# Recommender tower on one core: x_pair in 2 KB packets, chunk 0's loads together, a 128-row spread, idle transposes in two waits

## The chip, the cores and the metric

The kernel runs on one core of one Trainium2 chip. The metric is the device time of one execution in microseconds; the kernel before has a median of 543.13 us over 3 runs (542.85 to 1859.66). The profiled execution took 546.4 us, of which 544.6 us is the span from the first to the last instruction.

## What is computed

512 rows of 32 categorical fields are looked up in 32 tables of 16-wide fp32 embeddings. A compressed interaction network of three layers with 128 outputs each runs over them; its sums and 16 dense features go through three dense layers.

```python
e = jnp.stack([tbl_0[ids[:, 0]], ..., tbl_31[ids[:, 31]]], axis=1)      # (512, 32, 16)
x0, h = e, e
for i in range(3):
    z = (x0[:, :, None, :] * h[:, None, :, :]).reshape(B, F * G, E)
    y = relu(einsum('oc,bce->boe', Ws[i], z) + bs[i][None, :, None])
    if i != 2:
        x_keep, h = y[:, :64, :], y[:, 64:, :]
    else:
        x_keep = y
    xs.append(x_keep)
z = jnp.sum(jnp.concatenate(xs, axis=1), axis=2)
h = jnp.maximum(jnp.concatenate([z, dense_ctx], axis=1) @ W_top1 + b_top1, 0.0)
h = jnp.maximum(h @ W_top2 + b_top2, 0.0)
y = h @ W_top3
```

## The kernel before

The batch is cut into 16 chunks of 32 rows; a chunk's 32 rows times 16 components are the N = 512 columns of every big matmul. A layer of a chunk is a sum over channel products: VectorE (DVE) multiplies field tiles of x by h into z, TensorE (PE) multiplies z with the weights and adds up in a PSUM bank, ScalarE (ACT) applies relu and writes h for the next layer, twice (two halves of the partitions).

Layers 1 and 2 have 16 tiles of products (TILES), in 4 groups k of 4 tiles (GROUP). A step (layer, chunk, k) is one DVE product of 128x2048 and then the matmuls of its two pairs of tiles. A pair "by tensor" is two full fp32 matmuls (`unsplit`, L624), which the profile records as two records each: a whole step by tensor is 8 records. A pair in AT is split: ACT writes its high part (L520), GpSimd (POOL) its low part (L382), and PE runs six faster matmuls (`split`, L637). Layer 0 has one step per chunk, from x_rep and x_rot (L422). For chunk 0 nothing is split. PLAN lists the steps; every engine runs through it in this order. It begins with (1,0,0) to (1,0,3), (2,0,0), (2,0,1), (0,1,0), (2,0,2), (2,0,3), (1,1,0), (0,2,0), (1,1,1) to (1,1,3), and then turns through nine steps per chunk. The first steps of layers 1 and 2 of chunk 0 (HALVED) are made by DVE in two halves of 128x1024.

Data path of a chunk c: POOL issues 8 indirect gathers (L369) into `gathered`; SyncE (SP) stores them to `x_scratch` in DRAM (`store_x`, L295, two DMAs), and loads them back, replicated, as x_rep and x_rot for layer 0 (`load_x0`, L301 and L304, 5 DMAs of 256 KB over all 128 partitions) and as x_pair for layers 1 and 2 (`load_half`, L288). x_pair has two buffers, chunk mod 2. A group k of x_pair comes in two DMAs of 512 KB: half a = 0 goes to partitions 0 to 63, each of which gets the same four rows of x, half a = 1 to partitions 64 to 127 with four other rows. Since a group's four tiles stand side by side in a partition, each packet is 8 KB. All of SP's DMAs are written by hand in one order and go to one queue; the queue carries them out in that order.

The start is different. Chunk 0's gathered tile is loaded straight into `x_first`, which is 32 partitions of x_rot, and PE spreads it with five selecting matmuls (`spread_first`, L654) into PSUM; ACT copies the first bank to x_rep (L572), DVE makes the four product tiles of (0,0,0) from the banks (L461), and PE multiplies them (`start`, L660 and L664). Before it, PE turns the dense features (L669) and runs BUSY = 28 transposes of the identity that nobody reads (L677). Of chunk 0's x_pair, SP and ACT load the groups 0 and 1, one half each, as soon as store_x(0) has landed. SP then waits for chunk 1's gathers, stores chunk 1, and only then loads groups 2 and 3.

## Time and profile before

| what | us |
| --- | --- |
| median of 3 runs | 543.13 |
| profiled execution | 546.4 |
| its span | 544.6 |
| PE busy | 501.3 (92%) |
| DVE busy | 379.8 (70%) |
| POOL busy | 358.2 (66%) |
| ACT busy | 196.1 (36%) |

A busy PE is one with a matmul in flight. The page cuts the span into 40 slices of 13.6 us; the granted clock of TensorE is given in tenths of full speed. Times in the timeline are from the span's start.

### The profile page before, as it was taken

The page shows a single profiled execution, that of the slowest core. Times are in us where ns is not written, and L with a number is a line of the kernel's source. Part 1 is how long each engine was busy: PE and PEld are TensorE (multiplying, and loading weights), DVE is VectorE, ACT ScalarE, POOL GpSimd, SP SyncE. Part 2 cuts the span into 40 slices and gives each one's busy share as a digit, 9 for nine tenths or more (in the row PEclk, how much of TensorE's full clock was granted, in tenths as well). Part 3 has the DMA queues.
Part 4 walks back from the last instruction along what each step waited for, and adds up shares of the span by engine and source line. Part 5 has one row for each costly group of instructions (what it writes and reads, how often), then busy time and mean ns, then how long its engine had stood idle before and what let it go on. Part 6 is the DMA issues. An engine that isn't in the chain of part 4 may idle for free.

```text
span 544.6 us, 4268 instructions
## 1 busy us (share of the span) xinstructions
PE 501.3 (92%) x1446; PEld 273.1 (50%) x1446; DVE 379.8 (70%) x219; ACT 196.1 (36%) x253; POOL 358.2 (66%) x220
## 2 busy tenths in 40 slices
PE   0966769899999999999999999999999989899987
PEld 0622335355555555555545555555555554455555
DVE  1333964695959595959687786959595969867573
ACT  1210340434434443534253434334444424241242
POOL 5770347597969697887969696969697744715000
PEclk9897997999999999999999999999999999999999
DMA  7679599349998989797979797979798777350200
GB/s 230 131 164 255 150 243 233 105 110 250 219 247 184 250 182 238 167 235 160 228 158 231 166 227 161 221 166 243 159 220 199 171 196 159 89 110 9 76 0 0
DMA packets 33549, 94.50 MB, mean 174 GB/s; under 512 B 7844, under 2 KB 15012, under 8 KB 25080
## 3 DMA queue, kind: packets, MB, share of 16 engines
q1 hardware_dynamic: 27208, 91.87, 70.7%
q0 software_dynamic: 4096, 1.06, 1.7%
q10 hardware_dynamic: 2224, 1.31, 1.2%
q8 instruction: 11, 0.18, 0.2%
q14 instruction: 10, 0.08, 0.1%
HBM read 92.05 MB, written 2.10 MB: 173 GB/s over the span
## 4 chain that ended last, share of the span: by engine, by line
PE 75%; DVE 10%; issue 5%; DMA 4%; POOL 3%; ACT 2%; SPq 0%; DVEq 0%; ACTq 0%
PE acc L624 26%; PE acc L637 15%; PE spare L624 14%; PE x_bank L624 12%; DVE z L434 7%; PE x_bank L637 3%; POOL gathered L369 3%; PE spare L637 3%; DMA gathered<-in_table,rows_all 2%; DMA x_pair<-x_scratch 2%; DVE z L422 1%; DVE zl_parts L446 1%; DVE sum L451 1%; PE acc L642 1%; ACT h L534 1%
## 5 line engine op out<-in xcount | busy, mean ns | idle before, releaser
L382 POOL TENSOR_TENSOR z_low<-z,z_high 128x1024 fp32r<-128x1024 f32 x88 | 214.4, 2447 | 110.2 <-ACT z_high L520 109.4
L434 DVE TENSOR_TENSOR z<-h,x_pair 128x2048 f32<-128x2048 f32 (+1 forms) x65 | 144.8, 2248 | 115.8 <-ACT h L534 105.6
L624 PE MATMUL acc<-z,w_direct 128*128 128x512 f32 x384 | 175.0, 598 | 11.1 <-DVE z L434 11.1
L369 POOL DMA_INDIRECT gathered<-in_table,rows_all x128 | 143.6, 1122 | 33.3 <-issue 26.4
L520 ACT ACTIVATE z_high<-z 128x1024 fp32r<-128x1024 f32 x90 | 93.3, 1054 | 149.7 <-DVE z L434 127.7
L624 PEld LDWEIGHTS acc<-z,w_direct 128*128 128x128 f32 x384 | 72.9, 191 | 91.1 <-issue 71.9
L624 PE MATMUL spare<-z,w_direct 128*128 128x512 f32 x200 | 92.9, 603 | 11.2 <-DVE z L434 11.2
L624 PE MATMUL x_bank<-z,w_direct 128*128 128x512 f32 x200 | 89.9, 593 | 4.6 <-DVE z L434 4.6
L434 DVE TENSOR_TENSOR z<-h_odd,x_pair 128x2048 f32<-128x2048 f32 x32 | 72.3, 2278 | 8.1 <-ACT h_odd L534 8.1
L434 DVE TENSOR_TENSOR z<-h_even,x_pair 128x2048 f32<-128x2048 f32 (+1 forms) x33 | 72.3, 2213 | 5.2 <-ACT h_even L534 5.2
L624 PEld LDWEIGHTS spare<-z,w_direct 128*128 128x128 f32 x200 | 38.1, 193 | 55.6 <-issue 41.7
L624 PEld LDWEIGHTS x_bank<-z,w_direct 128*128 128x128 f32 x200 | 37.7, 189 | 44.4 <-issue 39.6
L637 PE MATMUL acc<-z_high,w_high 128*128 128x512 f32 x124 | 57.9, 548 | 0.0
L422 DVE TENSOR_TENSOR z<-x_rep,x_rot 128x2048 f32<-128x2048 f32 x15 | 44.2, 2945 | 0.0
L637 PE MATMUL acc<-z_high,w_low 128*128 128x512 f32 x124 | 39.2, 398 | 0.0
L637 PE MATMUL acc<-z_low,w_high 128*128 128x512 f32 x124 | 38.5, 392 | 0.0
L637 PEld LDWEIGHTS acc<-z_high,w_high 128*128 128x128 f32 x124 | 23.8, 192 | 23.9 <-issue 22.6
L534 ACT ACTIVATE h<-acc,columns 64x512 f32<-64x512 f32 x32 | 20.8, 652 | 37.2 <-PE acc L637 31.7
L534 ACT ACTIVATE kept<-acc,columns 64x512 f32<-64x512 f32 (+1 forms) x32 | 21.9, 683 | 30.3 <-PE acc L637 29.6
L534 ACT ACTIVATE h_even<-spare,columns 64x512 f32<-64x512 f32 x16 | 10.4, 652 | 45.5 <-PE spare L624 45.4
L637 PEld LDWEIGHTS acc<-z_low,w_high 128*128 128x128 f32 x124 | 23.6, 190 | 5.6
L637 PEld LDWEIGHTS acc<-z_high,w_low 128*128 128x128 f32 x124 | 23.6, 190 | 5.4
(144 smaller groups left out, 273.0 us busy)
## 6 DMA issues: line engine op xcount, KB each, us to landing
x_pair<-x_scratch SPq DMA_DIRECT2D x126, 512.0 KB, 7.2
x_rot<-x_scratch SPq DMA_DIRECT2D x60, 256.0 KB, 5.3
x_rep<-x_scratch SPq DMA_DIRECT2D x15, 256.0 KB, 5.1
w_direct<-in_W SPq DMA_DIRECT2D x2, 1024.0 KB, 8.6
gathered<-in_table,rows_all POOLq DMA_INDIRECT x128, 8.0
x_scratch<-gathered SPq DMA_DIRECT2D x32, 64.0 KB, 1.6
x_pair<-x_scratch ACTq DMA_DIRECT2D x2, 512.0 KB, 8.0
x_pair<-in_W_top SPq DMA_DIRECT2D x2, 512.0 KB
```

The lines of the kernel that those rows point to most:

```text
L369: pool.indirect_dma_start(gathered[:, c % X_SLOTS, j, :], None, table, bass.IndirectOffsetOnAxis(ap=rows.bitcast(U32), axis=0),).then_inc( ...
L382: nc.gpsimd.tensor_tensor(z_low[:, slot_of(pair)], products_of(pair), z_high[:, slot_of(pair)].bitcast(F32), ALU.subtract).then_inc(low_po ...
L422: nc.vector.tensor_tensor(z[:, step.group % Z_SLOTS], x_rep[:].unsqueeze(1).to_broadcast([P, GROUP, N]), x_rot[:], ALU.mult).then_inc(z_ma ...
L434: nc.vector.tensor_tensor(z[:, step.group % Z_SLOTS, first:end], h[:].unsqueeze(1).to_broadcast([P, end - first, N]), x_pair[:, chunk % 2, ...
L446: nc.vector.scalar_tensor_tensor(out=zl_parts[:], in0=zl_high[:].bitcast(F32), scalar=signs[:, 0:1], in1=zl_full[:], op0=ALU.mult, op1=ALU ...
L451: nc.vector.tensor_reduce(total[:, chunk * ROWS:(chunk + 1) * ROWS], kept.rearrange("p (b e) -> p b e", b=ROWS), AX.X, ALU.add).then_inc(m ...
L520: nc.scalar.activation(z_high[:, slot_of(pair)], products_of(pair), ACT.Copy).then_inc(high_made, 1)
L534: return nc.scalar.activation(dst, bank[rows, :], ACT.Relu, bias=bias[rows, layer:layer + 1])
L624: op = nc.tensor.matmul(bank_of(pair)[:], w_direct[:, first + i], products_of(pair)[:, i], start=i == 0 and pair is OPENS[pair.layer, pair ...
L637: op = nc.tensor.matmul(bank_of(pair)[:], w[:, at + i], zs[:, slot, i], start=part == i == 0 and pair is OPENS[pair.layer, pair.chunk], st ...
L642: nc.tensor.matmul(acc[0][:], wl_parts[:], zl_parts[:], start=False, stop=False)
```

## The change

1. x_pair is laid out `[P, 2, GROUP, GROUPS, N]`: tile i of group k stands at [i, k], so the four tiles of one transfer lie 8 KB apart and each partition gets four packets of 2 KB instead of one of 8 KB. What is computed and the number of DMAs are the same.
2. All four groups of chunk 0's x_pair are loaded as soon as store_x(0) has landed, half 0 by SP and half 1 by ACT. SP's loads of groups 2 and 3 behind store_x(1) are gone.
3. The spread has 128 rows: x_first is all 128 partitions, DVE first writes zeros to it, SP waits for that (`first_zeroed`), and `sel` is 128x640 instead of 32x640.
4. BUSY is 30 instead of 28, and WARM = 22 more transposes of the identity stand on PE ahead of (1,0,0) and of (2,0,0), into the bank that the step opens.

```diff
-BUSY = 28
+BUSY, WARM = 30, 22
-        x_pair = sb("x_pair", [P, 2, TILES, N])
+        x_pair = sb("x_pair", [P, 2, GROUP, GROUPS, N])
-        x_first = x_rot[0:FIELDS, 0, :]
+        x_first = x_rot[:, 0, :]
@@ load_half
-            eng.dma_start(x_pair[HALF * a:HALF * (a + 1), c % 2, GROUP * k:GROUP * (k + 1), :],
+            eng.dma_start(x_pair[HALF * a:HALF * (a + 1), c % 2, :, k, :],
@@ sync
+            sp.wait_ge(first_zeroed, 1)
             sp.wait_ge(gather_done[0], 16 * GATHERS)
-            sp.dma_start(x_first, gathered[:, 0].rearrange("p j e -> p (j e)")).then_inc(first_here, 16)
+            sp.dma_start(x_first[0:FIELDS], gathered[:, 0].rearrange("p j e -> p (j e)")).then_inc(first_here, 16)
             store_x(sp, 0)
             sp.wait_ge(x_stored[0], 32)
-            for k in range(2):
+            for k in range(GROUPS):
                 load_half(sp, 0, k, 0)
             store_x(sp, 1)
-            for k in range(2, GROUPS):
-                load_pair(0, k)
             sp.wait_ge(start_done, 1)
@@ vector
+            nc.vector.memset(x_first, 0.0).then_inc(first_zeroed, 1)
             dve.wait_ge(idx_here, 32)
@@ scalar
             act.wait_ge(x_stored[0], 32)
-            for k in range(2):
+            for k in range(GROUPS):
                 load_half(act, 0, k, 1)
@@ tensor
+            def keep_warm(bank, count):
+                for _ in range(count):
+                    nc.tensor.transpose(bank[:, 0:P], ident[:], ident[:])
             turn_dense()
-            for _ in range(BUSY):
-                nc.tensor.transpose(acc[0][:, 0:P], ident[:], ident[:])
+            keep_warm(acc[0], BUSY)
             spread_first()
             start()
             for n, step in enumerate(PLAN):
+                if step in HALVED:
+                    keep_warm(banks[step.layer][0], WARM)
```

On SP's queue, from the store of chunk 0 (`x_scratch<-gathered`) to the loads for chunk 1, this stood before:

```order
L295 DMA x_scratch<-gathered 128x128 x2
L288 DMA x_pair<-x_scratch 64x2048 x2
L295 DMA x_scratch<-gathered 128x128 x2
L288 DMA x_pair<-x_scratch 64x2048 x4
L301 DMA x_rep<-x_scratch 128x1x512
L304 DMA x_rot<-x_scratch 128x1x512 x4
L295 DMA x_scratch<-gathered 128x128 x2
L288 DMA x_pair<-x_scratch 64x2048 x4
```

and this stands now:

```order
L299 DMA x_scratch<-gathered 128x128 x2
L292 DMA x_pair<-x_scratch 64x4x512 x4
L299 DMA x_scratch<-gathered 128x128 x2
L305 DMA x_rep<-x_scratch 128x1x512
L308 DMA x_rot<-x_scratch 128x1x512 x4
L299 DMA x_scratch<-gathered 128x128 x2
L292 DMA x_pair<-x_scratch 64x4x512 x4
```

SP issues chunk 0's four half-0 loads ahead of chunk 1's store, and two of the six loads that it issued before are now ACT's.

On ACT, around the copy of the first spread bank into x_rep, this stood before:

```order
L566 ACTIVATE dense_high<-spare 51x512
L288 DMA x_pair<-x_scratch 64x2048 x2
L572 ACTIVATE x_rep<-x_bank 128x512
L528 ACTIVATE zl_full<-x_rep 128x512
L530 ACTIVATE zl_high<-zl_full 128x512
```

and this stands now:

```order
L570 ACTIVATE dense_high<-spare 51x512
L292 DMA x_pair<-x_scratch 64x4x512 x4
L576 ACTIVATE x_rep<-x_bank 128x512
L532 ACTIVATE zl_full<-x_rep 128x512
L534 ACTIVATE zl_high<-zl_full 128x512
```

Four DMA issues instead of two stand ahead of the copy.

On PE, from the spread's last matmul to layer 2 of chunk 0, this stands now (before, the rows of 22 were not there and the first row of transposes had 28):

```order
L662 MATMUL acc<-ident 128x128 x30
L658 MATMUL x_bank<-x_rot 128x512
L658 MATMUL acc<-x_rot 128x512 x2
L658 MATMUL h_even<-x_rot 128x512
L658 MATMUL h_odd<-x_rot 128x512
L668 MATMUL acc<-z 128x512 x4
L672 MATMUL acc<-zl_parts,wl_parts 128x512
L662 MATMUL spare<-ident 128x128 x22
L628 MATMUL spare<-z,w_direct 128x512 x16
L662 MATMUL x_bank<-ident 128x128 x22
L628 MATMUL x_bank<-z,w_direct 128x512 x12
```

The transposes of each new row lie between the end of one layer's matmuls and the first matmul of the next.

## Rows read from the trace of the kernel before

**Rows 1.** The page: busy time, then busy tenths and clock in 40 slices.
```profile
PE 501.3 (92%) x1446; PEld 273.1 (50%) x1446; DVE 379.8 (70%) x219; ACT 196.1 (36%) x253; POOL 358.2 (66%) x220
...
PE   0966769899999999999999999999999989899987
...
PEclk9897997999999999999999999999999999999999
```
**Rows 2.** Windows: stretch, length, busy (count) by engine, clock, DMA share, GB/s.
```profile
100.00:140.00 40.00, 36.82 (x104) 19.17 (x103) 31.80 (x17) 17.51 (x23) 34.08 (x22) 1.00 0.70 168
140.00:500.00 360.00, 356.69 (x1040) 196.02 (x1039) 280.28 (x148) 143.14 (x179) 270.82 (x152) 1.00 0.81 186
```
**Rows 3.** Chain of waits: start, duration; the same place two chunks apart.
```profile
184.82 6.87 PE acc L624 x16
...
243.07 6.87 PE acc L624 x16
```
**Rows 4.** Timeline of DVE from 28 us: start, duration, operation, [idle before <- releaser].
```profile
30.35 4.55 DVE L434 TENSOR_TENSOR z<-h,x_pair 128x1024 f32<-128x1024 f32 x3 [4.29 <-ACT h L534]
42.17 2.29 DVE L434 TENSOR_TENSOR z<-h,x_pair 128x2048 f32<-128x2048 f32 x1 [7.27 <-DMA x_pair<-x_scratch]
47.46 2.29 DVE L434 TENSOR_TENSOR z<-h,x_pair 128x2048 f32<-128x2048 f32 x1 [3.00 <-DMA x_pair<-x_scratch]
54.96 4.55 DVE L434 TENSOR_TENSOR z<-h_even,x_pair 128x1024 f32<-128x1024 f32 x3 [5.21 <-ACT h_even L534]
```
**Rows 5.** Timeline of PE: the two steps (1,0,0), (1,0,1), then (1,0,2), (1,0,3).
```profile
31.72 7.11 PE L624 MATMUL spare<-z,w_direct 128*128 128x512 f32 x16 [2.83 <-DVE z L434]
44.51 8.99 PE L624 MATMUL spare<-z,w_direct 128*128 128x512 f32 x16 [5.69 <-DVE z L434]
```
**Rows 6.** Timeline of SP's queue around chunk 0's loads.
```profile
16.61 1.05 SPq L295 DMA_DIRECT2D x_scratch<-gathered  x2
18.93 1.15 SPq L288 DMA_DIRECT2D x_pair<-x_scratch  x2
32.20 0.81 SPq L295 DMA_DIRECT2D x_scratch<-gathered  x2
33.05 2.37 SPq L288 DMA_DIRECT2D x_pair<-x_scratch  x4
```
**Rows 7.** Windows, columns as in Rows 2: full loads, chunk 0's x_pair, x0, x_pair.
```profile
5.00:8.00 3.00, 0.00 (x0) 0.00 (x0) 0.72 (x2) 1.52 (x3) 2.39 (x3) 1.00 1.00 377
20.00:30.00 10.00, 8.89 (x17) 3.33 (x15) 4.67 (x9) 4.14 (x9) 7.56 (x9) 0.83 0.97 213
268.00:272.00 4.00, 4.00 (x16) 2.82 (x15) 0.00 (x0) 1.99 (x3) 3.56 (x3) 1.00 0.99 211
291.00:293.00 2.00, 2.00 (x7) 0.84 (x5) 2.00 (x2) 0.00 (x0) 1.98 (x2) 1.00 1.05 381
```
**Rows 8.** Timeline of ACT from the first loads to layer 0's relu.
```profile
18.93 1.43 ACTq L288 DMA_DIRECT2D x_pair<-x_scratch  x2
20.46 0.60 ACT L572 ACTIVATE x_rep<-x_bank 128x512 f32<-128x512 f32 x1 [5.33 <-PE x_bank L654]
28.93 1.32 ACT L534 ACTIVATE h<-acc,columns 64x512 f32<-64x512 f32 x2 [5.32 <-PE acc L664]
```
**Rows 9.** Every DMA issue of L288: queue time ns min/median/max.
```profile
L288 SPq DMA_DIRECT2D x_pair<-x_scratch x126: 444/596/1644, 18.9 to 475.4; - x126
```
**Rows 10.** Windows of engine PE alone: busy (count), clock, DMA share, GB/s.
```profile
24.00:25.00 1.00, 1.00 (x2) 0.50 1.06 213
...
26.00:27.00 1.00, 1.00 (x2) 0.50 1.02 247
```
**Rows 11.** Windows of L677's transposes: PE busy, PEld busy, clock, DMA share, GB/s.
```profile
14.00:16.50 2.50, 2.20 (x11) 2.42 (x12) 1.00 0.09 6
17.00:18.50 1.50, 1.50 (x16) 1.50 (x15) 1.00 0.54 135
```
**Rows 12.** Windows, columns as in Rows 2: cold stretches after 40 us and 82 us.
```profile
40.90:47.70 6.80, 3.19 (x4) 1.50 (x5) 2.53 (x2) 0.00 (x0) 0.94 (x1) 0.50 1.01 258
81.90:88.70 6.80, 5.82 (x10) 3.28 (x11) 5.91 (x4) 1.06 (x1) 6.62 (x4) 0.50 1.04 246
```
**Rows 13.** Timeline of PE around 82 us.
```profile
82.88 3.78 PE L624 MATMUL acc<-z,w_direct 128*128 128x512 f32 x4 [5.18 <-DVE z L434]
```
**Rows 14.** Timeline of ACT: relu of (1,0), whose start is the shift's mark.
```profile
53.54 1.31 ACT L534 ACTIVATE h_even<-spare,columns 64x512 f32<-64x512 f32 x2 [22.59 <-PE spare L624]
```

More of the change, by code:

```diff
@@ L215, in dlrm_tower @@
         w_sym = z[:, 3].rearrange("p t n -> p (t n)")[:, 0:GROUP * P].rearrange("p (t o) -> p t o", o=P)
-        x_first = x_rot[0:FIELDS, 0, :]
-        sel = x_rot[0:FIELDS, 1:3].rearrange("p t n -> p (t n)")[:, 0:X0_LOADS * P].rearrange("p (t o) -> p t o", o=P)
-        hid2 = x_pair[:, 0, 4:6, :]
-        wt1 = x_pair[:, 0, 6:8, :]
-        wt2 = flat(x_pair[:, 0, 8:10, :])
-        wd = x_pair[0:COPIES * DENSE, 0, 10, :]
+        x_first = x_rot[:, 0, :]
+        sel = x_rot[:, 1:3].rearrange("p t n -> p (t n)")[:, 0:X0_LOADS * P].rearrange("p (t o) -> p t o", o=P)
+        free = x_pair[:, 0].rearrange("p i k n -> p (i k) n")
+        hid2 = free[:, 4:6, :]
+        wt1 = free[:, 6:8, :]
+        wt2 = flat(free[:, 8:10, :])
+        wd = free[0:COPIES * DENSE, 10, :]
         wt1_high, wt1_low = z_high[:, PAIR_SLOTS - 1], z_low[:, PAIR_SLOTS - 1]
@@ L252, in dlrm_tower @@
         first_here, sel_here, x0_here = sem("first_here"), sem("sel_here"), sem("x0_here")
-        spread, first_copied = sem("spread"), sem("first_copied")
+        first_zeroed, spread, first_copied = sem("first_zeroed"), sem("spread"), sem("first_copied")
         x_stored = [sem("x_stored_even"), sem("x_stored_odd")]
@@ L435, in products @@
                                             h[:].unsqueeze(1).to_broadcast([P, end - first, N]),
-                                            x_pair[:, chunk % 2, GROUP * k + first:GROUP * k + end, :],
+                                            x_pair[:, chunk % 2, first:end, k, :],
                                             ALU.mult).then_inc(z_made if end == GROUP else first_made, 1)
@@ L729 @@
     takes = np.concatenate([np.arange(FIELDS).repeat(GROUP).reshape(1, P), near.reshape(GROUP, P) % FIELDS])
-    sel = (np.arange(FIELDS)[:, None, None] == takes).astype(np.float32)
+    sel = (np.arange(P)[:, None, None] == takes).astype(np.float32)
     signs = np.zeros((P, 4), np.float32)
```

## The prediction

> **What bounds the kernel now.** I read the page first: PE is busy 92% of the span, but its slices are full only from about the eighth on; before that they fall to 6 and 7, and the clock digit falls in three places [rows 1]. The windows say the same with numbers: from 140 to 500 us PE is busy 356.69 of 360 us at full clock, while the DMA engines are 81% busy, and from 100 to 140 us PE is already busy 36.82 of 40 [rows 2]. The chain of waits repeats itself there: the same group of 16 records starts at 184.82 and at 243.07, so two chunks take 58.25 us and one 29.13 [rows 3]. So the long middle is PE's own work, and the change takes nothing from it. What can be won is the time until PE runs full, and a microsecond won there comes off the end in full, as long as the DMA keeps up.
>
> The ramp has one large hole. DVE makes (1,0,0) and (1,0,1) by 34.90, then waits 7.27 us for x_pair and 3.00 us more for the next group [rows 4]. PE's four steps of layer 1 therefore end only about 53.5, with 5.69 us of idling between the second and the third [rows 5], and ACT can start h_even at 53.54 [rows 14]. The loads that DVE waits for were issued at 33.05, since SP stood at the store of chunk 1 until 32.20, for chunk 1's gathers; chunk 0's own data had been in DRAM since 18.93, when the first two groups' loads went out [rows 6].
>
> **The change part by part.** The mark is the start of ACT's relu for layer 1 of chunk 0, 53.54 now. Two chains end in it.
>
> *The data.* All 8 halves are issued from 18.93 on. They are 8 x 512 KB = 4.19 MB. The two groups that are loaded there now move at 213 GB/s, two queues together [rows 7], so four groups need 19.7 us. Does the packet size change that rate? Loads that fill 128 partitions run at 377 GB/s with 8 KB packets (the weights) and at 381 with 2 KB packets (x_rep and x_rot), while x_pair, 64 partitions at a time, runs at 211 [rows 7]. So it is the partitions, not the packets, that halve the rate, and I keep 213. The Trainium skill says why (SBUF — State Buffer, Door 1: The DMA port swizzle): the partition number's bits choose one of 16 ports, and 64 adjoining partitions reach only 8 of them, which would be half of its ceiling of 435 GB/s. The trace agrees, with 211. By that rule the new packets bring nothing to the rate.
>
> I start the transfers 1.3 us after the issue (an estimate, from the 2.3 us between the issue of the stores at 16.61 and the loads that waited for them at 18.93 [rows 6], which has the data in it too) and 0.4 us later than now, for the larger sel (below): 20.6. Group 3 lands at 20.6 + 19.7 = 40.3, DVE needs 2.29 [rows 4], PE a step of 8 records, half of 6.87 = 3.43 [rows 3]; ACT starts at 40.3 + 2.3 + 3.5 = **46.2** with 0.1 for the hand-over. If the two queues fill both halves of the partitions at once, as 2 KB packets from two queues might, the rate could reach up to 381; then the data are there by 33 and this chain no longer decides.
>
> *The start.* Sel grows from 80 to 320 KB, and 246 KB at 377 GB/s are 0.65 us in front of the index loads; I take 0.4 for the gathers and everything behind them, and 0 to 0.65 as bounds. ACT issues four loads instead of two ahead of its copy to x_rep, 1.43 us for two [rows 8], so the copy moves from 20.46 by 1.43 + 0.4 to 22.3; bounds are 0.44 and 1.64 us for an issue [rows 9], thus 1.3 earlier and 3.7 later than that. A transpose takes 0.20 us early (11 in 2.20) and 0.094 to 0.107 later (16 or, without the two that the window cuts, 14 in 1.50) [rows 11], so two more cost 0.2 to 0.4, under ACT's delay. DVE's zeros stand ahead of its wait for the index, where it has nothing else to do, and SP's new wait on them is over long before chunk 0's gathers, the wait right behind it; both cost nothing. If the clock stays up, the matmuls of `start`, which now run at 0.50, the 1.2 GHz level, between 24 and 27 us with two records in a microsecond [rows 10] instead of one each 0.43 (6.87 over 16, [rows 3]), save 3 x 0.5 = 1.5 us. PE was busy all the time before that drop, with transposes and matmuls of 32 rows; whether 128 rows keep the level no row shows, so the saving is 0 to 1.5, and I take it in full, since no other drop in this trace lacks an idle stretch ahead of it [rows 5, 12, 13]. Together: +1.8 - 1.5 = +0.3, so that DVE starts (1,0,0) near 30.65. From there PE alone needs 1.37 until its first matmul (31.72 - 30.35, [rows 4, 5]) and 4 x 3.43 = 13.7: it ends at **45.7**, and ACT starts at 45.8. If the clock falls all the same, 47.3; if each issue on ACT takes 1.64, 49.5.
>
> The later of the two chains decides: 46.2, or 53.54 - 46.2 = **7.3 us** earlier.
>
> *The transposes in the waits.* PE idles 2.83 us ahead of (1,0,0) [rows 5]. 22 transposes at 0.094 to 0.107 are 2.1 to 2.4 us and fit; at the slow 0.20 they are 4.4 and would hold PE back 1.6 us. Here a rule speaks against the change. The row: 11 transposes took 2.20 us, and from 17 us on 16 took 1.50, with nothing else on PE in between [rows 11]; so the clock rose while PE did transposes alone. The Trainium skill says (TensorE: Matmul & The Clock Gate, Part 4) that transposes do not count as busy for the clock gate; by it the fillers would not hold the clock, which is a rival below. The trace does not agree. The gain of the fillers is small all the same, because in this trace the clock did not fall in either gap of 2.8 us; it fell after 40.9 and after 81.9 [rows 12], behind idle stretches of 5.69 and 5.18 us [rows 5, 13]. The first of these goes with the loads and is in the sum; the second is of the dependencies of chunk 1, moves along with all the rest, and stays. I book 0 for the fillers; -1.6 and, for a drop avoided, +1.7 are the bounds.
>
> *What is late next.* SP's queue now has the store of chunk 1 behind four x_pair loads, so it lands near 40.5 instead of right after 32.20; x_rep and x_rot of chunk 1 follow, five issues of about 0.6 us [rows 9] and 1.31 MB at 381 GB/s = 3.4 us, thus by about 47. DVE needs them behind (2,0,1), which now would end near 54.96 + 4.55 - 7.3 = 52.2 [rows 4]. 5 us to spare, so nothing.
>
> *The middle.* A chunk moves 4.19 MB of x_pair, 19.8 us at 211 GB/s, and all its DMA is 0.81 x 29.13 = 23.6 us [rows 2, 3]. It becomes the bound when x_pair takes 29.13 - 3.8 = 25.3 us, at 165 GB/s, 22% below now. At 2 KB the loads on 128 partitions lose nothing, so I book 0.
>
> Sum: -7.3 us against the profiled execution, whose span of 544.6 lies in 546.4. The median is 543.13, 3.3 less than it; the removed wait has no reason to be shorter there, so the same 7.3 us come off: 543.13 - 7.3 = **535.8**.
>
> **The rivals.**
> - *More than that.* Data at up to 381 GB/s and no delay on ACT would leave PE's chain at about 43.9 (30.35 - 1.5 + 1.37 + 13.7), and 9.6 us won: 533.5. If besides the cold stretch at 82 us stays away, whose ten records take 5.82 us [rows 12], up to 2.9 us more: 530.6. For: two queues could fill both halves. Against: they already do for groups 0 and 1, at 213 [rows 7], and the idle stretch at 77 to 83 is untouched.
> - *Less.* ACT's four issues stall or the clock still falls in `start`: the mark at 47.3 to 49.5, 4.0 to 6.2 us won, 537 to 539. Against a long stall: the median issue is 0.596 [rows 9].
> - *The fillers cost.* Transposes do not keep the clock, and 22 of them at 0.20 us end 1.6 us after DVE's first half: the mark at 45.8 + 1.6 = 47.4, 6.1 us won, 537.0. Against it stands the clock that rose under transposes [rows 11]. This is what the rule of the Trainium skill named above would do here.
> - *Slower, one mechanism.* 64 partitions with 2 KB packets run below 165 GB/s, for example if each packet's own cost adds to the shared port's time. No row shows such packets. At 150 GB/s a chunk would need 4.19/0.150 + 3.8 = 31.7 us, 2.6 more than PE, over some 13 chunks 34 us: 543.13 - 7 + 34 = 570. It decides from 165 GB/s down. Against: packets of 2 KB cost nothing on 128 partitions, and a port that is waited for has time to hide an overhead.
> - *No effect.* The early loads starve chunk 1's gathers or x_rot as much as they gain: 541 to 543. For: gathers share the engines with x_pair. Against: POOL issues its gathers on its own queue in both cases, and x_rot has 5 us to spare.
>
> **How the numbers follow.** 7.3 us are 1.3%, below the 2% (10.9 us) that a measurement of this kernel tells from no change. Forecast (5.5 to 8.5 us won) 0.56; more 0.18, of which 0.10 past 10.9 us, where the clock at 82 us has to help; less 0.10; fillers that cost 0.04; no effect 0.04; slower 0.08. The range leaves out the slow case, no effect and the last of the gains: 531.5 to 541.0. Faster 0.10, within 2% 0.82, slower 0.08.
>
> **What would show it.** In the new timeline DVE should wait for x_pair under 3 us in all (10.27 now), ACT should start h_even near 46, the x_pair windows should stand at 210 GB/s, the `start` matmuls at full clock, and the middle at 58.25 us for two chunks. The forecast is wrong if the DMA share of the middle goes to 1, if x_pair's windows show 300 GB/s or more, if DVE waits for x_rot at (0,1,0), or if x_rep's copy starts after 25 us.

## The result, and the profile after

The changed kernel took 538.23 us (median of 4 runs, 538.08 to 539.00); the kernel before, run beside it, 545.31 us (median of four: 542.85, 543.13, 547.49 and one of 1859.66). The ratio of the two without that last one is 0.9881 (95% interval 0.9850 to 0.9912): 1.2% less, thus within 2%, as forecast. The forecast was 535.8 us with a range of 531.5 to 541.0. The ratio makes the gain 6.5 us. Profiled execution against profiled execution it is larger: 546.4 us before (span 544.6), 538.08 after (span 536.3), 8.3 us.

The page of the changed kernel, with the same columns as [rows 1]:

```profile
PE 502.8 (94%) x1492; PEld 276.9 (52%) x1492; DVE 380.1 (71%) x220; ACT 196.1 (37%) x253; POOL 357.9 (67%) x220
...
PE   0899859899999999999999999999999899899987
...
PEclk9999979899999999999999999999999999999999
```

From the second slice to the sixth PE's tenths are 8, 9, 9, 8, 5, where [rows 1] have 9, 6, 6, 7, 6. Two dips of the clock in the first four slices are gone.

The timeline of DVE from 28 us answers [rows 4]:

```profile
30.06 4.55 DVE L438 TENSOR_TENSOR z<-h,x_pair 128x1024 f32<-128x1024 f32 x3 [1.64 <-ACT h L538]
35.06 2.29 DVE L438 TENSOR_TENSOR z<-h,x_pair 128x2048 f32<-128x2048 f32 x1 [0.45 <-DMA x_pair<-x_scratch]
38.20 2.29 DVE L438 TENSOR_TENSOR z<-h,x_pair 128x2048 f32<-128x2048 f32 x1 [0.85 <-DMA x_pair<-x_scratch]
46.86 4.55 DVE L438 TENSOR_TENSOR z<-h_even,x_pair 128x1024 f32<-128x1024 f32 x3 [6.36 <-ACT h_even L538]
```

The waits for x_pair, 7.27 and 3.00 us before, are 0.45 and 0.85 us. Layer 2 of chunk 0 starts at 46.86 instead of 54.96, 8.10 us earlier, with (1,0,0) only 0.29 earlier. So the gain arises between these two steps. PE's timeline, against [rows 5], and behind it the idle stretch of [rows 13]:

```profile
28.44 2.56 PE L662 MATMUL spare<-ident 128*128 128x128 f32 x22
31.43 13.97 PE L628 MATMUL spare<-z,w_direct 128*128 128x512 f32 x32 [0.42 <-DVE z L438]
45.24 2.57 PE L662 MATMUL x_bank<-ident 128*128 128x128 f32 x22
48.23 7.11 PE L628 MATMUL x_bank<-z,w_direct 128*128 128x512 f32 x16 [0.42 <-DVE z L438]
...
74.80 3.78 PE L628 MATMUL acc<-z,w_direct 128*128 128x512 f32 x4 [5.18 <-DVE z L438]
```

All four steps of layer 1 now run without a break, 32 records in 13.97 us. The 22 transposes take 2.56 us and leave 0.42 idle. The last matmul of the spread and the matmuls of `start` on PE, and the product on DVE that `start` needs first, were these before:

```profile
22.32 1.02 PE L654 MATMUL h_odd<-x_rot 32*128 32x512 f32 x2
23.26 5.40 PE L660 MATMUL acc<-z 128*128 128x512 f32 x8
21.09 1.28 DVE L461 TENSOR_TENSOR z<-x_rep,acc 128x512 f32<-128x512 f32 x2 [5.19 <-ACT x_rep L572]
```

and are these now:

```profile
23.52 1.02 PE L658 MATMUL h_odd<-x_rot 128*128 128x512 f32 x2
24.67 3.70 PE L668 MATMUL acc<-z 128*128 128x512 f32 x8
23.93 1.29 DVE L465 TENSOR_TENSOR z<-x_rep,acc 128x512 f32<-128x512 f32 x2 [6.41 <-ACT x_rep L576]
```

The mark, ACT's relu of (1,0) [rows 14], and the copy ahead of the start [rows 8]:

```profile
20.00 3.19 ACTq L292 DMA_DIRECT2D x_pair<-x_scratch  x4
23.30 0.60 ACT L576 ACTIVATE x_rep<-x_bank 128x512 f32<-128x512 f32 x1 [6.55 <-PE acc L658]
...
45.44 1.32 ACT L538 ACTIVATE h_even<-spare,columns 64x512 f32<-64x512 f32 x2 [14.77 <-PE spare L628]
```

The mark moved from 53.54 to 45.44. SP's queue, against [rows 6], then the windows of chunk 0's loads and of an x_pair load in the middle, against [rows 7], and the long middle, against [rows 2]:

```profile
19.99 2.64 SPq L292 DMA_DIRECT2D x_pair<-x_scratch  x4
31.33 0.80 SPq L299 DMA_DIRECT2D x_scratch<-gathered  x2
39.47 0.56 SPq L305 DMA_DIRECT2D x_rep<-x_scratch  x1
```
```profile
21.00:27.00 6.00, 5.88 (x15) 2.41 (x14) 3.07 (x6) 3.08 (x7) 4.48 (x6) 1.00 1.00 209
28.00:36.00 8.00, 7.58 (x35) 4.66 (x34) 5.91 (x6) 1.99 (x3) 5.98 (x7) 1.00 1.06 316
260.00:264.00 4.00, 4.00 (x17) 2.87 (x16) 0.00 (x0) 2.08 (x4) 3.67 (x3) 1.00 1.07 209
140.00:492.00 352.00, 348.70 (x1016) 191.42 (x1015) 272.55 (x143) 141.13 (x177) 263.16 (x148) 1.00 0.84 185
```

The middle is what it was: PE busy 348.70 of 352 us, and the chain of waits repeats after 58.25 us, as in [rows 3] (176.49 and 234.74 us). The DMA share there rose from 0.81 to 0.84. The loads of x_pair alone still run at 209 GB/s in the middle (211 before). But chunk 0's, on two queues, ran at 209 only for the first six microseconds and then at 316.

### The profile page after: what moved, and what is told of

Read it like the earlier page. It is cut to its first block, busy times and chain, and to the rows that moved or that the text cites. A ratio compares the mean times of both kernels' runs of the same rounds, so it can differ in the third digit from the quotient of the medians.

```text
span 536.3 us, 4362 instructions
## 1 busy us (share of the span) xinstructions
PE 502.8 (94%) x1492; PEld 276.9 (52%) x1492; DVE 380.1 (71%) x220; ACT 196.1 (37%) x253; POOL 357.9 (67%) x220
## 4 chain that ended last, share of the span: by engine, by line
PE 80%; DVE 9%; issue 4%; ACT 2%; DMA 1%; POOL 1%; ACTq 1%; SPq 0%; DVEq 0%
PE acc L628 27%; PE spare L628 15%; PE acc L641 15%; PE x_bank L628 12%; DVE z L438 6%; PE x_bank L641 3%; PE spare L641 3%; POOL gathered L372 1%; DVE z L426 1%; DVE zl_parts L450 1%; ACT h L538 1%; PE acc L668 1%; PE acc L646 1%; DMA row<-in_row 1%; DVE sum L455 1%
## 5 line engine op out<-in xcount | busy, mean ns | idle before, releaser
L628 PE MATMUL spare<-z,w_direct 128*128 128x512 f32 x200 | 90.7, 593 | 2.1 <-DVE z L438 2.1
L628 PEld LDWEIGHTS x_bank<-z,w_direct 128*128 128x128 f32 x200 | 37.7, 189 | 41.4 <-issue 36.6
```

The source lines that it names most:

```text
L628: op = nc.tensor.matmul(bank_of(pair)[:], w_direct[:, first + i], products_of(pair)[:, i], start=i == 0 and pair is OPENS[pair.layer, pair ...
```

## The experiments

A word on the place first. On the first chip the kernel before had taken 543 to 547 us. Beside the first eight experiments it took 563 to 567 us, and the parts of the change gained nothing there; beside the last four it took 544. What makes those executions long hides the change, so some of the experiments ask for that cause. A figure that stays useful in both cases is the *rest*: the span less the start of DVE's (1,0,0). It is 544.6 - 30.35 = 514.3 us for the kernel before and 536.3 - 30.06 = 506.2 for the changed one on the first chip.

**The parts apart** (all but the 128-row spread, which was never taken alone). The first kernel is the one before with this:

```diff
@@ sync (the same k range in scalar)
-            for k in range(2):
+            for k in range(GROUPS):
                 load_half(sp, 0, k, 0)
             store_x(sp, 1)
-            for k in range(2, GROUPS):
-                load_pair(0, k)
```

> The kernel before with one edit: all four groups of chunk 0's x_pair are loaded at once, half 0 by SP and half 1 by ACT, still in 8 KB packets. Theory (the wait for groups 2 and 3 is the whole gain): 6 to 8 us less than before, ACT's relu for layer 1 of chunk 0 starts at 45 to 47.5 instead of 53.54, and the x_pair windows of this load stand at 210 to 240 GB/s. Rival (8 KB packets spoil it, since the gathers and the store of chunk 1 wait behind them): 0 to 3 us less than before, and DVE waits for x_rep and x_rot at (0,1,0).

The second is the kernel before with only the new layout (`x_pair` as `[P, 2, GROUP, GROUPS, N]` and its uses):

> The kernel before with one edit: x_pair laid out so that its packets are 2 KB, loads in the old order. Theory: within 1 us of before; x_pair windows at 210 to 215 GB/s, DMA share of the middle 0.81 to 0.86. Rival (packets alone help, since gathers land sooner): 3 us or more faster. Second rival (more packets cost): slower by 2 us or more, with SP's issues of L288 stalling and the margin of x_rep and x_rot in the ramp gone.

The third is the changed kernel with the old layout:

> The changed kernel with x_pair's old layout, so 8 KB packets. Theory (only chunk 0's two-queue load runs faster with 2 KB, 310 instead of 213 to 240 GB/s, and PE is nearly the bound there): 0 to 1.5 us slower than the changed kernel, DVE's waits for x_pair at (1,0,2) and (1,0,3) grow from 1.3 us in all to 2 to 5. Rival (packets carry the gain): 4 us or more slower than the changed kernel.

The fourth is the changed kernel without the transposes in the two waits:

```diff
-BUSY, WARM = 30, 22
+BUSY, WARM = 30, 0
```

> The changed kernel with WARM = 0, so without the 22 transposes in each of the two waits. Theory (the clock also held through gaps of 2.8 us in the kernel before): within 1 us of the changed kernel. Rival (the clock falls behind a gap now and then): a stretch at 0.50 behind one of the gaps and 1.5 to 3.5 us slower in some executions.

Measured, on one chip: the kernel before 563.74 us; loads at once 565.29 (ratio 1.0009, 0.9975 to 1.0044); 2 KB layout alone 563.66 (0.9998, 0.9965 to 1.0031); changed with 8 KB 564.08 (1.0004, 0.9979 to 1.0029); changed without the idle transposes 564.02 (1.0015, 0.9981 to 1.0048). All four equal the kernel before, and that one lies 18 us above the first chip. Only the second expectation (within 1 us of before) was met, and that says nothing, since no product waited for x_pair in any of the four. DVE's timeline of the fourth shows where:

```profile
46.69 0.69 DVE L465 TENSOR_TENSOR z<-x_rep,acc 128x512 f32<-128x512 f32 x1 [31.28 <-remote]
...
55.03 8.95 DVE L438 TENSOR_TENSOR z<-h,x_pair 128x1024 f32<-128x1024 f32 x5 [3.10 <-ACT h L538]
```

and PE's and ACT's of the third:

```profile
23.39 1.02 PE L657 MATMUL h_odd<-x_rot 128*128 128x512 f32 x2
48.96 5.91 PE L667 MATMUL acc<-z 128*128 128x512 f32 x8 [24.55 <-DVE z L464]
```
```profile
47.59 0.60 ACT L575 ACTIVATE x_rep<-x_bank 128x512 f32<-128x512 f32 x1 [32.59 <-remote]
```

PE has issued the five products of the spread by 24.4 us, as on the first chip, but ACT, which waits for the first of them, starts at 47.59 instead of 23.30. In the trace's record of semaphores the five counts on `spread` come at 47.50 to 47.67 us; in the changed kernel on the first chip they come at 21.13, 21.98, 22.84, 23.70 and 24.56, each at the end of its product. When at last DVE reaches (1,0,0) at 55 us, all of x_pair has been there for more than ten microseconds, early issue or late. That hides what the change does.

Two things can be read from the four all the same. The rests are 505.4, 505.5, 505.6 and 507.4 us: the first chip's kernel before has 514.3, and all four have the changed kernel's 506.2 within 1.2, the second one too, which has the old place of the loads. So the difference between the kernels is their x_pair wait and little else; where the data are there before the start is, the kernel before has nothing left to lose. And the windows from 28 to 36 us, in which nothing but loads and gathers runs, give the rate of the two queues on one chip, for 8 KB packets (third kernel) and 2 KB packets (fourth):

```profile
28.00:36.00 8.00, 0.00 (x0) 0.00 (x0) 0.00 (x0) 0.00 (x0) 6.17 (x7) 0.60 1.03 225
```
```profile
28.00:36.00 8.00, 0.00 (x0) 0.00 (x0) 0.00 (x0) 0.00 (x0) 5.99 (x7) 0.50 1.06 315
```

The packets do change the rate where two queues fill the two halves of the partitions: 315 against 225 GB/s. Of all traces in which the eight loads go out at 19 to 20 us, the five with 8 KB packets have 225 to 253 GB/s over this stretch and the five with 2 KB packets 315 to 335. Where one queue fills the halves in turn, no such difference shows (209 GB/s with 2 KB and 211 with 8 KB in the middle).

**The first one once more, twice**, in the hope of a run whose start isn't held up:

> The kernel before with one part of the change alone: all eight halves of chunk 0's x_pair are issued at once on SP's and ACT's queues, with the old layout (8 KB packets), the 32-row spread and no idle transposes in the two waits. Theory A (the early issue carries the whole gain, and the two queues move 8 KB packets no slower than 2 KB ones, about 310 GB/s once both have work): the two x_pair waits of (1,0,0) (7.27 and 3.00 us before) fall below 1 us each, the first ReLU of (1,0) on ACT moves from 53.54 to about 45, and the kernel gains 7.5 to 9.5 us; since it doesn't pay the 1.05 us of the 128-row selection, it may end level with the changed kernel or up to 1 us ahead, less the slow clock in the start (about 1.5 us). Theory B (the layout is what lets the two queues overlap; 8 KB packets to 64 partitions stay at 213 GB/s): the last group lands near 40, waits of 1.5 to 3 us stay, and the gain is 5 to 7 us. Theory C (TensorE is the chain at the start, and without the filler transposes its clock falls in the wait, so the tile L628 x32 takes more than 14 us): a gain of 4 to 6 us with the waits gone.

> The kernel before with one part of the change alone: all eight halves of chunk 0's x_pair are issued at once; old layout with 8 KB packets, 32-row spread, no idle transposes in the two waits. It is the kernel of the first and fifth experiment again, for a run in which TensorE's counts of the spread come on time. Theory A (the place in the queues is the whole gain): groups 2 and 3 are issued by 22 us instead of 33.05 us, DVE's waits of 7.27 and 3.00 us shrink below 1 us each, TensorE's chain sets the first ReLU of (1,0); that chain lacks the 128-row selection (about 1 us earlier) and has the slow clock in the start and perhaps in the tile L628 x32 (1.5 us and more): ReLU at 44.5 to 47 us, total 536 to 540 us, within 1.5 us of the changed kernel's 538.2. Theory B (without 2 KB packets the two queues move only 213 GB/s): the last group lands at about 40 us, waits of 1 to 3 us stay, total 539 to 542 us. Theory C (as in the changed kernel, the two queues together move over 300 GB/s in the second part whatever the packets): the last group lands by 38 us.

Measured: 564.02 us (kernel before 563.39; ratio 1.0004, 0.9969 to 1.0039) and 562.83 us (563.20; 0.9982, 0.9948 to 1.0016), the second on another chip. The counts of the spread came at about 47 us in both. They decide nothing on the time, since no product waited for x_pair. On the rate they do: with 8 KB packets the two queues moved 253 and 244 GB/s from 28 to 36 us, not over 300.

**What holds the counts back.** While they are missing, GpSimd issues gathers without a pause (to 42.9 us) and both queues load. Two versions of the changed kernel have each one of these put behind the counts:

```diff
@@ gpsimd
             for c in range(AHEAD):
+                if c == 2:
+                    pool.wait_ge(spread, X0_LOADS)
                 for j in range(GATHERS):
                     gather(c, j)
```

> The changed kernel, in which GpSimd's gathers of chunk 2 and of later chunks wait until all five products of the spread (L658) are counted. On this chip the kernel before takes 563.7 us and not 543 to 545, and in the traces of the four experiments so far TensorE issues the five products at 19.4 to 24.4 us, but their count on the semaphore `spread` arrives at 41 to 48 us instead of 21.1 to 24.6; all that time GpSimd issues gathers (until 42.9 us) and the two queues load chunk 0's x_pair (until about 42). Theory A (the gathers' traffic beside the loads holds the count back): with GpSimd stopped at about 25 us the count arrives by 32 us, and the time falls by 12 to 20 us, to 545 to 552 us. Theory B (the loads of x_pair alone hold it back): the count stays at 41 to 48 us and the time at 562 to 566 us or some us above. Theory C (neither; the count is late by a fixed time): the same as B, which the second kernel of this pair tells apart.

```diff
@@ sync and scalar, ahead of chunk 0's load_half
+            sp.wait_ge(spread, X0_LOADS)
+            act.wait_ge(spread, X0_LOADS)
```

> The changed kernel, in which all loads of chunk 0's x_pair (both queues) wait until all five products of the spread are counted. Theory A (the gathers hold the count back): count at 41 to 48 us, then 15 us more for the loads: about 575 us. Theory B (the loads hold it back): the count arrives at 21 to 25 us as on the first chip, the loads run from 25 to 45 us, DVE's (1,0,0) waits for the groups as in the kernel before, and the time is 543 to 549 us. Theory C (a fixed delay, whatever the traffic): count at 41 to 48 us.

Measured, one execution each, on one chip, beside the kernel before at 567.33 us: with late gathers 545.25 us, with late loads 567.48 us. Timelines of GpSimd and ACT in the first of the two, then of ACT in the second:

```profile
24.05 0.95 POOL L372 DMA_INDIRECT gathered<-in_table,rows_all  x1 [0.31 <-issue]
28.37 0.95 POOL L372 DMA_INDIRECT gathered<-in_table,rows_all  x1 [3.37 <-remote]
```
```profile
28.03 0.60 ACT L578 ACTIVATE x_rep<-x_bank 128x512 f32<-128x512 f32 x1 [11.95 <-remote]
```
```profile
50.60 0.60 ACT L578 ACTIVATE x_rep<-x_bank 128x512 f32<-128x512 f32 x1 [35.16 <-issue]
```

GpSimd stops at 25.0 us, and the five counts come together at 27.94 to 28.11, 2.9 us later. Without the stop most of them come at 46.5 to 48.1 us, some 5 us after GpSimd's last gather (which ends at 41.4 to 42.9), whether the queues load x_pair meanwhile or not (second kernel: 46.49 to 47.34). So the gathers decide, as theory A had it, and the loads have no part in it. Each of the two is one execution, so this is strong evidence but not more. By what road a gather on GpSimd's queue can hold up a count of PE, and why it does so in some runs only, these two don't show; on the first chip the gathers ran just as densely, and the counts were on time. Once the start is over it doesn't come back: in the first of the two GpSimd gathers again from 28.37 to 45.8 us, and layer 1 of chunk 0 runs beside it in the 13.97 us that it has elsewhere.

**The gathers stopped earlier.** The changed kernel and the kernel before, with the same wait one chunk sooner:

```diff
@@ gpsimd
             for c in range(AHEAD):
+                if c == 1:
+                    pool.wait_ge(spread, X0_LOADS)
```

> The changed kernel, with one line more: GpSimd gathers chunk 0, then waits until all five products of the spread are counted, and only then goes on to chunk 1. The look before this one, with the wait ahead of chunk 2, brought the count from 47 to 27.9 us and the time from 567.33 to 545.25 us on the same chip. Theory A (the count is held back while gathers follow each other without a pause, and released when they stop): GpSimd stops at about 15 us, the count comes at 21.1 to 24.6 us as on the first chip, (1,0,0) starts at 30 us, and the time is that of the changed kernel on the first chip, 537 to 540 us, some 25 us under the kernel before on this chip. Chunk 1's x_rep and x_rot then land at about 50 us (use at 52), so up to 1 us can be lost there. Theory B (the count is late by about 3 us even without gathers beside it, or the start's own counts are now the ones held back, since chunk 1's gathers fall on them): 541 to 548 us.

> The kernel before, with the same line: GpSimd gathers chunk 0, then waits for the five counts of the spread. The pair measures the change where the start isn't held up. In the kernel before, SP issues groups 2 and 3 of chunk 0's x_pair behind its store of chunk 1's x (issued at 32.20 us, the groups at 33.05 us and later), which waits for chunk 1's gathers. Theory A (what the change removes is this place in SP's queue): here chunk 1's gathers end 7 us later, so the groups are issued at about 39.5 us, DVE's third product of (1,0,0) starts at about 48.5 us instead of 42.17, and the time is 548 to 553 us: the changed kernel gains 12 to 15 us on this one, and not the 7 to 8 of the first chip. Theory B (the loads were limited by the rate of the queues, about 213 GB/s, and not by when they are issued): the third product stays at 42 to 43 us, and the time is 543 to 546 us, 7 to 8 us over the changed kernel.

Beside these, on the same chip as the last two, the kernel before took 544.06 us: nothing was held up. Measured: changed kernel with the wait 544.20 us (537.79 to 545.58 in 10 runs; ratio 0.9982, 0.9947 to 1.0017), kernel before with the wait 550.04 us (1.0102, 1.0070 to 1.0134). The second, DVE and SP:

```profile
44.40 2.29 DVE L436 TENSOR_TENSOR z<-h,x_pair 128x2048 f32<-128x2048 f32 x1 [11.17 <-DMA x_pair<-x_scratch]
```
```profile
35.62 2.42 SPq L288 DMA_DIRECT2D x_pair<-x_scratch  x4
```

Later gathers of chunk 1 make chunk 0's third product later: the loads go out at 35.62 instead of 33.05, the wait grows from 7.27 to 11.17 us, and the kernel takes 6.0 us more. That is theory A: the place behind the store of chunk 1 is the cause (I had expected the issue at 39.5 and the product at 48.5; the gathers landed sooner). Of the 6.0 us the two traces show 3.8 (spans 548.4 and 544.6): the mark is 2.8 later, at 56.30, and 1.0 more goes in layer 2 of chunk 0, where the clock is at its 1.2 GHz level from 58.4 to 65.2 us. The other 2.2 lie between the traced execution of the kernel before on the first chip (546.4) and the runs here. The first shows something that I had not looked for. Its start is as good as the changed kernel's, the mark at 45.06, and yet nearly 6 us are lost again before 110 us. Its rest is 542.6 - 29.68 = 512.9 us. The places are DVE's (0,3,0) and PE's next idle time:

```profile
104.29 4.38 DVE L428 TENSOR_TENSOR z<-x_rep,x_rot 128x2048 f32<-128x2048 f32 x1 [3.50 <-DMA x_rot<-x_scratch]
```
```profile
111.58 4.83 PE L630 MATMUL spare<-z,w_direct 128*128 128x512 f32 x7 [5.83 <-DVE z L440]
```

and this is SP's queue there, the wait's kernel first and the changed kernel second:

```profile
96.20 0.55 SPq L305 DMA_DIRECT2D x_rep<-x_scratch  x1
```
```profile
57.39 17.07 SPq L292 DMA_DIRECT2D x_pair<-x_scratch  x12
...
92.47 0.55 SPq L305 DMA_DIRECT2D x_rep<-x_scratch  x1
```

SP comes to chunk 3's x_rep and x_rot 3.7 us later, so x_rot is late: it lands at 104.2. In the changed kernel its last load is issued at 95.0 us and lands 4.3 us later, at 99.3; DVE needs it at 100.23. The kernel before had 104.2 against 108.95. In these two traces the margin has shrunk from 4.7 to 0.9 us, so the changed kernel can stand right in front of a new wait, and every delay of SP's queue in the ramp beyond that costs. How much is left differs from execution to execution: in the first kernel of the next pair, which differs by a wait that stops nothing, x_rot lands at 96.6 and is needed at 99.93. The rate at which the one queue loads before it differs too, 217 GB/s from 75 to 85 us in the changed kernel, 208 where the wait stood ahead of chunk 1, and 226 in that next kernel.

**The last pair: does the place of the loads carry it all?** The wait ahead of chunk 2, which costs nothing where the counts are on time, in the changed kernel and in the kernel before with the loads at once (the edits of the late gathers and of the first experiment):

> The changed kernel with GpSimd's gathers of chunk 2 and later behind the five counts of the spread (the first of the two looks again, now timed in rounds). In a run where the counts come on time (24.6 us) GpSimd reaches this wait at about 25 us and loses nothing: the time is the changed kernel's, 537 to 540 us, 5 to 8 us under the kernel before. In a run where the kernel before takes 563 us, the counts come at about 28 us instead of 47: (1,0,0) starts at 36 to 38 us, from there to the end 505.5 to 507.5 us as in all six kernels whose x_pair had landed by then, so 543 to 547 us, 17 to 20 us under the kernel before. A rival: the late gathers of chunks 2 and 3 make x of chunk 3 late, as in the kernel whose wait stood ahead of chunk 1; then the rest from (1,0,0) takes 509 to 513 us.

> The kernel before with the loads of chunk 0's x_pair at once and the same wait of GpSimd ahead of chunk 2: no 2 KB packets, 32-row spread, no idle transposes. Theory A (the place of the loads is the whole gain; layout, rows and idle transposes are worth under 1.5 us together): from the start of (1,0,0) to the end 505.5 to 508 us, with waits for x_pair under 1 us each, and a time within 1.5 us of the kernel sent with it. Theory B (2 KB packets are needed for over 300 GB/s of the two queues; with 8 KB the last group lands at 39 to 41 us): where (1,0,0) starts at 30 us, waits of 1 to 3 us and 2 us over the other kernel; where it starts at 37 us, no wait, but the landing times show the rate. Theory C (the idle transposes keep the clock up): 1.5 to 3 us over the other kernel, in a stretch at half clock between 30 and 60 us.

On this chip nothing was held up; the kernel before took 544.24 us. Measured: changed kernel with the wait 538.33 us (0.9891, 0.9866 to 0.9917), loads at once with 8 KB packets, 32 rows and no idle transposes 538.58 us (0.9911, 0.9877 to 0.9944). In both traces GpSimd gathers on without a pause at the wait, so it is not the wait that gains. The place of the loads (part 2 of the change) alone has the gain; the other three parts together add 0.25 us, which these runs don't tell from nothing. The traces are finer. DVE of the first, then of the second:

```profile
34.31 2.29 DVE L440 TENSOR_TENSOR z<-h,x_pair 128x2048 f32<-128x2048 f32 x1 [0.33 <-DMA x_pair<-x_scratch]
37.32 2.29 DVE L440 TENSOR_TENSOR z<-h,x_pair 128x2048 f32<-128x2048 f32 x1 [0.72 <-DMA x_pair<-x_scratch]
```
```profile
31.67 2.29 DVE L434 TENSOR_TENSOR z<-h,x_pair 128x2048 f32<-128x2048 f32 x1 [0.23 <-DMA x_pair<-x_scratch]
36.20 2.29 DVE L434 TENSOR_TENSOR z<-h,x_pair 128x2048 f32<-128x2048 f32 x1 [2.25 <-DMA x_pair<-x_scratch]
40.32 2.29 DVE L434 TENSOR_TENSOR z<-h,x_pair 128x2048 f32<-128x2048 f32 x1 [1.83 <-DMA x_pair<-x_scratch]
```

and the windows of both, first with 2 KB packets, then with 8 KB, with the second's stretches at half clock behind it:

```profile
28.00:36.00 8.00, 7.58 (x34) 4.52 (x33) 6.24 (x4) 1.99 (x3) 6.17 (x7) 1.00 1.07 328
```
```profile
28.00:36.00 8.00, 5.55 (x9) 2.41 (x10) 4.65 (x3) 1.65 (x3) 6.17 (x7) 0.79 1.03 237
...
75.90:79.30 3.40, 3.40 (x5) 1.33 (x6) 3.40 (x3) 0.91 (x1) 3.24 (x3) 0.50 1.04 231
31.50:34.90 3.40, 3.40 (x6) 1.35 (x5) 2.29 (x1) 0.00 (x0) 2.66 (x3) 0.51 1.04 251
48.60:52.00 3.40, 2.80 (x4) 1.28 (x5) 3.40 (x3) 1.26 (x2) 0.00 (x0) 0.50 1.06 248
```

With 8 KB packets the two queues move 237 GB/s, group 3 lands at 40.3 us instead of about 37.3, the waits sum to 4.31 us, and the clock falls to its 1.2 GHz level at 31.5 and at 48.6 us, where it stays at 2.4 GHz with the idle transposes and the early data. The mark is at 46.41 against 44.80 us. Here the clock decides and the data stand close behind: PE's 32 records of layer 1 run without a break, but take 15.92 instead of 13.97 us, and 3.4 us at half clock are 1.7 of that (an estimate). By group 3's data alone the mark would come at 40.32 + 2.29 + 3.43, some 46.0 us. So of the 1.61 us no single part can be said to bring most: the idle transposes with 8 KB packets, or the 2 KB packets without them, were not run where nothing is held up. Of these 1.61 us, 0.84 are left at (1,2,0) (88.75 against 87.91), since the clock of the 2 KB kernel is down for 6.8 us from 72.5 on and that of the other for only 3.4 us from 75.9 on.

The wait ahead of chunk 2 gives a kernel that beats both: as fast as the changed one where the counts come on time (538.33), and 22 us under the kernel before, 545.25 against 567.33, in the one pair of executions where they don't. The changed kernel itself was never timed where the counts are late.

## Why the prediction was right, and where it wasn't

- **What bounds the kernel** held: the long middle didn't move, and a microsecond won at the mark came off the end. 8.10 at the mark, 8.3 in the whole.
- **The data.** The step that failed is "it is the partitions, not the packets, that halve the rate, and I keep 213". The 40.3 us that came of it for group 3 is what 8 KB packets give (40.3 in the last experiment). With 2 KB packets group 3 landed at 38.2, since the two queues moved 316 GB/s from 28 us on; the prediction had named 300 GB/s or more as a sign against it. The rows weighed against each other were loads on 128 partitions and on 64 one after the other; two queues on two halves at once stood only in the row with 213, with 8 KB packets, and I took that for a limit of both. The rival "two queues fill both halves" was right in its mechanism. That the forecast stood all the same is luck in part: it named the data's chain (46.2) as the one that decides, and PE's chain, which did decide, lay only 0.4 us below it. The port table of the Trainium skill (SBUF — State Buffer, Door 1: The DMA port swizzle) gives the two halves different ports, 8 each; taken by itself that leaves room for more. A line on another page speaks against that: transfers to disjoint halves of the partitions "serialize" (DMA: Bandwidth & Descriptors, Rules for kernel authors). Here that nearly holds with 8 KB packets (225 to 253 GB/s against 211 to 242 of one queue), and not with 2 KB packets (315 to 335 against 208 to 226).
- **The start, and the chain that decides.** PE's chain was forecast at 45.8 and the mark came at 45.44. (1,0,0) started at 30.06, forecast 30.65: two terms were off, and in opposite directions. ACT's copy to x_rep came at 23.30, 2.84 us later than before, where the forecast had 1.8 (22.3). Of that, 1.07 is the later issue of chunk 0's loads (20.00 against 18.93; the larger sel was booked at 0.4 us with 0.65 as its bound), and 1.76 the four issues (3.19 us against 1.43). But not all of it stands on the path. Before, the first product was ready at about 21.8 (one takes 0.69 us), and PE came to `start` at 23.26 only, behind the spread; so the copy could slip 1.4 us for nothing, which the sum left out. Now the product is ready at about 24.6, the spread ends at 24.5 and `start` begins at 24.67, 1.41 later: ACT's copy and PE's spread reach it within 0.1 us of each other, and the copy is the later one (the chain of waits runs through ACT's four issues, the copy and the product). `start` then took 3.70 us instead of 5.40, so it saved 1.70 where 1.5 was booked, and 1.70 less 1.41 is the 0.29 by which (1,0,0) came earlier. Over all traces that show both, chunk 0's loads go out at 19.30 to 20.01 us in six with 128 rows and at 18.57 to 19.38 in seven with 32, in the mean 0.63 later. That 128 rows have earned the full clock is not shown: in both kernels of the last four that have 32 rows `start` took 3.70 us too. One bound in the working was off by itself: four issues at 0.44 us put the copy 1.1 us earlier and not 1.3.
- **The idle transposes.** Booked at 0 with the bounds -1.6 and +1.7. 22 took 2.56 us each time, a little over my 2.1 to 2.4, and still fit. The fourth experiment against the third puts them at nothing in the time (564.02 against 564.08; they differ in the packets as well), though its rest is 1.7 us longer. For the clock they do count: in the six traces that have them it stayed at 2.4 GHz across both waits (in the changed kernel from 17.8 to 72.4 us), and of the six without them whose data were early it fell during or right behind one of the waits, or both, in three. That is six traces against six, and so a sign more than a proof. The Trainium skill says that transposes don't count for the clock gate (TensorE: Matmul & The Clock Gate, Part 4); by it the clock should have fallen as often with them as without, and these traces don't agree.
- **What is late next.** x_rep and x_rot of chunk 1 were forecast for 47 us against 52.2; they landed at 47.3 and were needed at 51.92. Right, but the check ended too early: the tight place is chunk 3's x_rot, with 0.9 us to spare, which no step of the prediction named.
- **The middle.** 209 GB/s for x_pair, 58.25 us for two chunks, DMA share 0.84: right, and the slower rival with under 165 GB/s fell. The packets cost something else, single issues that take up to 4.9 us where [rows 9] have 1.6 at most (2.2 in the last experiment, with 8 KB as well). It did not delay what follows: chunk 3's x_rep is issued at 92.47 here and at 92.32 there. The same view:

```profile
L292 SPq DMA_DIRECT2D x_pair<-x_scratch x124: 573/616/4946, 20.0 to 467.3; - x124
```

- **The base.** The sum took 7.3 us off 543.13. The miss is 2.4 us, and it can't be split exactly, because the median of 545.31 beside the changed kernel has the execution of 1859.66 in it. By the ratio the gain was 6.5 us, and by the last pair (544.24 against 538.33, with the wait ahead of chunk 2) 5.9; so about 1 us of the miss is the gain and the rest the base. The traces gave 8.3 because the traced execution of the kernel before, 546.4 us, was longer than any of its 22 runs beside the last four experiments (542.60 to 545.96). "The removed wait has no reason to be shorter there" is therefore not borne out; what is shorter in those executions no trace shows.

## What to carry to other kernels

When an engine waits for a load, look first at what stood ahead of the load's issue in its queue: here a store that waited for something else, and moving the issues of two groups was worth nearly the whole 6 us (544.24 to 538.58). Two things that are equal in the time can be far apart in margin, so after a ramp has been shortened, go through every later transfer of that queue and note how much is left. And try a wait on an engine that issues many small indirect DMAs while the start's critical counts are due. Here it cost nothing ahead of chunk 2 (538.33 us); one chunk sooner it cost the changed kernel all of its gain (544.20), so its place has to be measured.

## What the runs showed of the hardware

- Two queues that fill opposite halves of the partitions moved 315 to 335 GB/s with 2 KB packets and 225 to 253 with 8 KB (five traces each, all from 28 to 36 us). One queue that fills the halves in turn moved 209 and 211 in the windows of the middle, and from 75 to 85 us 208 to 226 with 2 KB and 225 to 242 with 8 KB (three traces each). For the first six microseconds the 2 KB loads of the changed kernel ran at 209 as well; why they then speed up was not tried.
- In some executions, on three chips, PE's counts of five matmuls came up to 27 us after the matmuls, in five of eight traces all within 0.2 us of each other, and nearly all only when GpSimd had stopped issuing gathers (the earliest at 41.0, with gathers until 42.9). A stop of the gathers at 25 us brought them to 28 us, in one execution. The same chip had executions with and without it. What passes between the two engines stays open.
- TensorE's clock fell to its 1.2 GHz level in or right behind the idle stretch of some 5.2 us, for 6.8 us in nine traces and for 3.4 in five, and not by version: three runs of one kernel (the loads at once) have 3.4, 6.8 and 6.8. The shorter one gave back 0.8 us in the last experiment.
